# Attention block and mixture of experts on one core: the split of the batches into two expert segments, the spacing of the last stage, the number of padding tiles and the mask of the maxima are changed

## The reference, cut to what matters

```python
# attention: 16 heads of 8 columns, causal
scores = Q @ K.T / sqrt(8);  scores = where(k > q, -1e6, scores)
attn = softmax(scores) @ V
x = layernorm(x + attn @ Wo + bo)
# experts: 8 of them, the best two for each row, hidden width 512
xn = layernorm(x) * gamma + beta
p = softmax(xn @ Wg.T);  top1, top2 with weights p1/(p1+p2), p2/(p1+p2)
y = sum over the two: weight * (gelu(xn @ W1[e] + b1[e]) @ W2[e] + b2[e])
x = layernorm(x + y)
```

## Time and profile before

| what | value |
|---|---|
| median of 3 runs | 992.43 us (990.83 to 999.39) |
| the profiled execution: its time, its span | 994.34 us, 992.5 us |
| PE, DVE, ACT, POOL busy | 88%, 75%, 68%, 66% of the span |
| attention (the scores end) | about 20 to 650 us |
| tiles without the last stage | 658 to 880 us |
| tiles beside the last stage | 880 to 962 us |
| last stage alone | 969 to 992.5 us |

### The profile page before, as it was taken

The page is one execution under the profiler, slowest core; times in us unless marked ns, Lnnn a source line. Parts: engine busy times, 40 slices in busy tenths (PEclk is TensorE's granted clock), DMA queues, the critical chain, the costliest instruction groups (busy, mean ns, idle before and its releaser), DMA issues.

```text
span 992.5 us, 29037 instructions
## 1 busy us (share of the span) xinstructions
PE 873.5 (88%) x9185; PEld 566.2 (57%) x9185; DVE 740.1 (75%) x2029; ACT 677.9 (68%) x1434; POOL 653.6 (66%) x907
## 2 busy tenths in 40 slices
PE   4689899998999989999999999769999999998960
PEld 2334444444444444544444444359999988998860
DVE  1877779888988888888888888855554555458867
ACT  1277687777787777877777877746666555667763
POOL 6243555778678777777787786667767656556652
PEclk9799999999999999999999999989999999999995
DMA  7614635636446355345354342253233323266644
GB/s 198 194 66 158 176 92 165 175 107 203 123 146 203 100 172 167 103 155 171 99 165 147 101 145 61 79 143 87 79 81 89 86 75 89 74 206 193 209 110 146
DMA packets 169379, 132.50 MB, mean 134 GB/s; under 512 B 52938, under 2 KB 155377, under 8 KB 169104
## 3 DMA queue, kind: packets, MB, share of 16 engines
q1 hardware_dynamic: 156880, 112.48, 38.5%
q0 software_dynamic: 8704, 17.06, 5.1%
q10 hardware_dynamic: 3648, 1.12, 0.5%
HBM read 71.55 MB, written 61.15 MB: 134 GB/s over the span
## 4 chain that ended last, share of the span: by engine, by line
PE 37%; POOL 8%; issue 6%; ACT 5%; DVE 5%; DMA 1%; ACTq 1%; SPq 0%; DVEq 0%; POOLq 0%
PE ring L1235 12%; PE ring L1251 11%; PE ps_v L1171 3%; POOL probs L666 2%; PE ring L1108 2%; DVE negmax L1282 2%; ACT probs L798 2%; PE ring L1139 2%; POOL rs L732 1%; POOL rows_d L708 1%; PE ps_v L1225 1%; ACT probs L937 1%; DVE probs L1624 1%; PE ring L1154 1%; ACT vpad L922 1%
## 5 line engine op out<-in xcount | busy, mean ns | idle before, releaser
L1282 DVE TENSOR_REDUCE negmax<-ring 128x2 f32<-128x1024 f32 (+3 forms) x512 | 409.5, 814 | 70.5 <-PE ring L1154 67.5
L798 ACT ACTIVATE probs<-ring 128x768 f32<-128x768 f32 (+1 forms) x384 | 334.7, 878 | 114.0 <-PE ring L1108 107.9
L666 POOL TENSOR_SCALAR_AFFINE_SELECT probs<-probs 128x512 f32<-128x512 f32 x256 | 162.8, 639 | 159.5 <-ACT probs L798 157.7
L922 ACT ACTIVATE vpad<-ring,b_s 128x128 f32<-128x128 f32 x576 | 164.5, 370 | 113.5 <-PE ring L1235 111.1
L716 POOL DMA_INDIRECT y_d<-vpad,xs x144 | 146.3, 1016 | 99.1 <-DVE vpad L1593 54.9
L1171 PE MATMUL ps_v<-probs,vpad 128*32 128x512 f32 (+3 forms) x2048 | 180.2, 441 | 8.3 <-POOL probs L666 8.3
L1235 PE MATMUL ring<-vpad,w_t 128*128 128x128 f32 x1152 | 156.0, 279 | 8.7 <-ACT vpad L945 5.8
L1251 PE MATMUL ring<-qarea,vpad 128*128 x1152 | 155.0, 278 | 3.3 <-issue 3.0
L1235 PEld LDWEIGHTS ring<-vpad,w_t 128*128 128x128 f32 x1152 | 141.7, 194 | 11.1 <-ACT vpad L945 7.2
L708 POOL DMA_INDIRECT rows_d<-xn,slot x128 | 128.6, 1005 | 28.4 <-issue 25.1
L1251 PEld LDWEIGHTS ring<-qarea,vpad 128*128 128x128 f32 x1152 | 140.0, 192 | 7.8 <-issue 6.5
(11 more groups left out here) (190 smaller groups left out, 1170.0 us busy)
## 6 DMA issues: line engine op xcount, KB each, us to landing
kside<-qk_d SPq DMA_DIRECT2D x32, 512.0 KB, 5.5
qk_d<-qarea SPq DMA_DIRECT2D x32, 384.0 KB, 2.7
xs<-rows_d SPq DMA_DIRECT2D x144, 66.0 KB, 1.9
qk_d<-qarea SPq DMA_DIRECT2D x32, 256.0 KB, 2.4
qarea<-qk_d SPq DMA_DIRECT2D x16, 512.0 KB
qodd<-qk_d SPq DMA_DIRECT2D x16, 512.0 KB
probs<-y_d SPq DMA_DIRECT2D x16, 512.0 KB, 4.5
xin<-L_attn_x SPq DMA_DIRECT2D x16, 256.0 KB, 3.8
```

The lines of the kernel that those rows point to most:

```text
L666: pool.affine_select(out=diag, in_=diag, pattern=[[0, 4], [1, P]], compare_op=ALU.is_ge, fill=0.0, base=0, channel_multiplier=-1).then_inc ...
L798: nc.scalar.activation(of_unit(h // 2, part), ring[:, 2 * part % 3, :, (0, P, P)[part]:S], ACT.Exp, scale=SCALE).then_inc(sem("exp_done"), 1)
L922: ins = nc.scalar.activation(ht[:, n % 4, c, :], ps_a[:, n % 4, c * P:(c + 1) * P], ACT.Gelu_apprx_tanh, bias=b1_s[:, bass.ds(e, 1), c:c + ...
L1282: ins = nc.vector.tensor_reduce(negmax[:, n // 6 % 2, qb, s:s + 2], ring[:, (2 * n + 1) % 3, :, c0:c0 + nk], AX.X, ALU.max, negate=True)
```

## The change

It has four parts.

1. `FIRST` is (0, 11, 16) in place of (0, 12, 16): segments of 11 and 5 batches.
2. `TILES` has 7 padding tiles for each segment in place of 8: 88 + 7 = 95 and 40 + 7 = 47, 142 tiles in all, where 104 + 40 = 144 stood.
3. The last stage of batches 0 to 10 starts every 4 steps, from step 95 + 4 = 99; that of batches 11 to 15 every 3 steps, from step 147. The fifth of the late batches uses the buffers of the first of them.
4. Each half of a diagonal block is masked by 64 columns, not 128. The quarter that this leaves out (first 64 queries, second 64 keys) is masked through the spare rows: a row that is 1 for the queries of a first half meets one that is the large negative number for the keys of the same block's second half. `fill` becomes two tiles (in `x2` and `xc`), and their second rows are computed at the start by one iota, three small instructions and two copies. These rows are in both score products.

```diff
-    FIRST = (0, NB - 4, NB)
+    FIRST = (0, NB - 5, NB)
-    TILES = [n * TOPK // P + E for n in SEG]
+    TILES = [n * TOPK // P + E - 1 for n in SEG]
...
-        LAST0, LAST_STEP, LAST_PARTS = TILE0[1] + 4, 3, 12
-        STEPS = range(2 * PAIRS, LAST0 + LAST_STEP * NB + LAST_PARTS)
+        LAST0, LAST_PARTS = TILE0[1] + 4, 12
+        LAST_AT = [LAST0 + 4 * b if b < FIRST[1] else NT + 5 + 3 * (b - FIRST[1]) for b in range(NB)]
+        STEPS = range(2 * PAIRS, LAST_AT[-1] + LAST_PARTS)
...
-            b, rest = divmod(n - LAST0 - part, LAST_STEP)
-            return b if rest == 0 and 0 <= b < NB else None
+            return LAST_AT.index(n - part) if n - part in LAST_AT else None
...
-                             fill[:, :] if what else across(fill[:, 1], 2)).then_inc(sem(f"filled{par}"), 16)
+                             fill[what][:, :]).then_inc(sem(f"filled{par}"), 16)
...
-            sp.wait_ge(sem("fill_set"), 2)
+            sp.wait_ge(sem("fill_set"), 4)
...
-                if b < FIRST[1]:
+                if not FIRST[1] <= b < FIRST[1] + 4:
                     load_x2(b)
...
-                if b is not None and b + 4 < FIRST[1]:
+                if b is not None and (b + 4 < FIRST[1] or FIRST[1] <= b < NB - 4):
                     load_last(b + 4)
                 b = last_stage(n, 3)
-                if b is not None and FIRST[1] <= b + 4 < NB:
+                if b is not None and b < FIRST[1] <= b + 4:
                     load_x2(b + 4)
                 if n == NT + 1:
-                    for b in range(FIRST[1], NB):
+                    for b in range(FIRST[1], FIRST[1] + 4):
                         load_last(b)
...
+            pool.iota(past_i[:, 0], pattern=[[1, 2 * QB]], base=2 * P, channel_multiplier=-2).then_inc(
+                sem("past_rows"), 1)
...
-                        past = pastb[rows, at:at + P]
+                        past = pastb[rows, HALF:P]
                         if n % 3 == 2:
-                            to = to.rearrange("p (a n) -> p a n", n=P)[:, 0:QB:QB - 1, :]
-                            past = past.unsqueeze(1).broadcast_to([HALF, 2, P])
+                            to = to.rearrange("p (a n) -> p a n", n=P)[:, 0:QB:QB - 1, HALF * c:HALF * (c + 1)]
+                            past = past.unsqueeze(1).broadcast_to([HALF, 2, HALF])
                         else:
-                            c1 = (QB - 1 - n % 3) * P
-                            to = to[:, c1:c1 + P]
+                            c1 = (QB - 1 - n % 3) * P + HALF * c
+                            to = to[:, c1:c1 + HALF]
...
-            nc.vector.memset(fill[:, 0], 1.0).then_inc(sem("fill_set"), 1)
-            nc.vector.memset(fill[:, 1], 0.0).then_inc(sem("fill_set"), 1)
+            nc.vector.memset(fill[1][:, 0], 1.0).then_inc(sem("fill_set"), 1)
+            nc.vector.memset(fill[0][:, 0], 0.0).then_inc(sem("fill_set"), 1)
+            dve.wait_ge(sem("past_rows"), 1)
+            nc.vector.tensor_scalar(past_i[:, 1], past_i[:, 0], 2 * HD - 1, None, ALU.bitwise_and).then_inc(
+                sem("past_rows"), 1)
+            dve.wait_ge(sem("past_rows"), 2)
+            for what in range(2):
+                nc.vector.tensor_scalar(past_f[:, what], past_i[:, 1], float(what), NEG if what else 1.0, ALU.is_equal,
+                                        ALU.mult).then_inc(sem("past_rows"), 1)
+            for what in range(2):
+                dve.wait_ge(sem("past_rows"), 3 + what)
+                nc.vector.tensor_copy(fill[what][:, 1].rearrange("p (j n) -> p j n", n=HALF),
+                                      along(past_f[:, what], HALF)).then_inc(sem("fill_set"), 1)
```

More of the change, by code:

```diff
@@ L203, in build_program @@
         flat = probs[:, :, :].rearrange("p r n -> p (r n)")
-        fill = xc[:, :, :].rearrange("p q d -> p (q d)").bitcast(BF16).rearrange("p (r n) -> p r n", r=2)
+        fill = [t[:, :, :].rearrange("p q d -> p (q d)").bitcast(BF16).rearrange("p (r n) -> p r n", r=2)
+                for t in (x2, xc)]
+        past_i = sb("past_i", [P, 2, 2 * QB], I32)
+        past_f = sb("past_f", [P, 2, 2 * QB])
         y_t = flat[:, 0:8 * S].rearrange("p (r n) -> p r n", r=4)
@@ L295, in expert_steps @@
             return (n, n + 1)
-        LAST0, LAST_STEP, LAST_PARTS = TILE0[1] + 4, 3, 12
-        STEPS = range(2 * PAIRS, LAST0 + LAST_STEP * NB + LAST_PARTS)
+        LAST0, LAST_PARTS = TILE0[1] + 4, 12
+        LAST_AT = [LAST0 + 4 * b if b < FIRST[1] else NT + 5 + 3 * (b - FIRST[1]) for b in range(NB)]
+        STEPS = range(2 * PAIRS, LAST_AT[-1] + LAST_PARTS)
+        assert LAST_AT == sorted(set(LAST_AT))
         def copied(n):
```

## The result

| | median | runs | ratio to the kernel before |
|---|---|---|---|
| before | 996.06 us (990.83 to 1001.06) | 20 | |
| changed | 985.1 us (978.84 to 993.68) | 20 | 0.9897, 95% 0.9872 to 0.9922 |

The change brings 10 to 11 us. The forecast was 975, range 966 to 984: too low by 10, and just outside the range. A part of that is the ground it stood on: the three runs that were shown had a median of 992.43, twenty have 996.06. Against these, a forecast of 17.5 us less would have been 978.6; 6.5 us did not come.

The account below looks back on a forecast made before the run. Bounds: a chain of waits through several engines in attention, VectorE's queue beside the last stage. Terms -8.2 - 12.6 + 2.6 + 0.7 = -17.5 took 994.34 us to 976.8; 1.9 lower for the median gave 975, range 966 to 984.

Parts of the forecast that it names:

- What bounds the kernel: Attention: a chain of waits, 38.3 us a batch, 15 of them over GpSimd; beside the last stage: VectorE's queue, W1 copy last.
- Tiles and last stage, -12.6: Tile 99 to the last tile: two tiles fewer and four steps a batch take 82.9 us, not 95.5; 12.6 us less.
- I take 1.95 for all: Tiles beside the last stage: each of 40 steps was priced at 1.95 us, between 1.90 and 1.99.
- the variance's step would be at 1.90: Last stage beside tiles: variance with two factors is shorter than four additions, so its step takes 1.90 us.
- Rival 3: Last stage beside tiles still costs 0.98 us a batch, ScalarE or the wait for factors being late; 983 us, chance 0.10.
- Its mark: Tiles beside the last stage: a step over 2.2 us in each batch would prove the rival of an unchanged last-stage cost.
- The mask, -8.2: Attention: 64-column masks shorten TensorE's pieces on the chain by 0.55 us a batch, over fifteen batches 8.2 us less.
- rival 4: Attention: TensorE's granted clock falls as the mask streams half the columns, making the kernel slower, 1021 us; chance 0.04.
- the clock stayed at 1.00 where TensorE was busy 93%: Attention: reason given against a clock fall, with the change taking only some 5% off TensorE's work.
- Five batches at the end, +2.6: End of the kernel: one more batch at 3.95 us, less 1.3 us now standing in a wait; 2.6 us more.
- Counters, +0.7: Attention: three small VectorE instructions saving counters move from iteration 15 to 14, onto the chain; 0.7 us more.
- The start, 0: Kernel start: five more small VectorE instructions delay the fill transfers by under 1 us, within 12 us of cover; no cost.

Follow-up runs that it names:

- e3: Changed kernel with VectorE copying W1 of tile n+2 directly behind the result of tile n-1, ahead of additions, statistics and factors; ratio 0.9828 to the kernel before.
- e4: Changed kernel without ScalarE's normalising of batches 0 to 10, except four columns, so their output is not computed; ratio 0.9898 to the kernel before.
- e12: Kernel before with W1 of tile n+2 copied directly behind the result of tile n-1; ratio 0.9939 to the kernel before.
- e14: Changed kernel with 128-column masks, each mask product made twice, in units 12 to 14 of a batch's 24; ratio 0.9875 to the kernel before.
- e16: Changed kernel with W1 copied behind the result, normalising moved later, expert loads ahead of the x2 store, doubled 128-column masks in units 12 to 14; ratio 0.9766, 972.83 us.
- e2: Changed kernel with the old 128-column masks and old fill rows; ratio 0.9912 to the kernel before.
- e7: Changed kernel with 128-column masks in all units, the spare rows kept; ratio 0.9957 to the kernel before.
- e1: Kernel before with only the 64-column masks and their spare rows added; ratio 0.9938 to the kernel before.
- e5: Changed kernel with W1 of tile n+2 copied behind the result of tile n-1, and batches 0 to 10 normalised in parts 10 and 11, not 8 and 9; ratio 0.9861.
- e13: Changed kernel run again unaltered, for comparison on the same chip; ratio 0.9907 to the kernel before.
- e10: Kernel before with the expert-weight and padding-tile loads issued earlier, ahead of the store of x2; ratio 0.9935 to the kernel before.
- e15: Changed kernel with expert loads ahead of the x2 store, and 128-column masks with each product made twice in units 12 to 14; ratio 0.9857 to the kernel before.
- e9: Changed kernel with the expert-weight and padding-tile loads issued earlier, ahead of the store of x2; ratio 0.9892 to the kernel before.

## Why the prediction was partly wrong

*What bounds the kernel.* Right for attention: the chain with its GpSimd part, and TensorE's pieces in the rest (undisturbed batches at 37.7 us, as forecast). For the tiles the engine was right (VectorE's queue, the W1 copy last) and e3, e4 and e12 show it.

*Tiles and last stage, -12.6.* This step failed: "I take 1.95 for all". It took the additions, behind which the W1 copy still stood, to be nearly free. The engine was right and the size wrong; the term measured -6.7 in the profile (-6.2 to -8.7 in the eight profiles that have the changed kernel's order of tiles and all of its work).

The 1.95 came from a single step of additions alone, 1.99 us, behind tile 110, which had itself waited 0.92 us. In that wait VectorE had caught up: the copy for the product at 886.64 had ended 0.5 us before it. In the steady state nobody catches up, since TensorE alone needs 1.90. Each step with additions costs what the result, 1.04 us of additions, 0.42 us of copy and the passing on take, and a short step does not give it back. The statement that the variance's step would be at 1.90 failed too: it took 1.94 and 1.90 in the first two batches, then 2.03 to 2.17, though the copy was in time there. Of the 5.9 us, 39 steps of 2.07 are 4.8; the step of 2.88 is 0.9, and the first two are 0.2.

Rival 3 priced this at 0.98 us a batch, and 8.36 - 7.58 = 0.78 us was measured. Its mark, a step over 2.2 us in each batch, held in the first two batches (3.15 and 2.88) and in four others (2.21 to 2.31), and not in the rest. It was nearer than the forecast (90.7 us for T, against 88.8 measured and 82.9 forecast), with the cause on VectorE and not where it was put.

*The mask, -8.2.* Price and mechanism of a piece were right: 0.06 and 0.11 us a piece, 37.7 us a batch. The second pair of products follows the first by 28 ns in the median, where it was 56, and by 56 where it was 109. The Trainium skill, "TensorE: Matmul & The Clock Gate", section "LDWEIGHTS (loading the stationary operand)", with its 107 ns for a load of 128 columns would have kept the pieces as they were, and they halved. A load's own record in these groups is 94 ns long, near that figure, but the product that needs it starts 27 ns behind the load's start: the length of a load is not the distance between products.

What failed is the sum over the batches, and with it the reason against rival 4: "the clock stayed at 1.00 where TensorE was busy 93%". Rival 4 had the right mechanism with the wrong measure on both sides. The share of a 100 us stretch says nothing here. It is the poorest place of a batch that the added work of e14 to e16 mended, where 2.1 to 2.3 of 3.40 us had become 1.84. And the clock does not fall for all batches but in two or three of sixteen, and costs 1.4 to 1.9 us each time.

With the expert loads where they were, A is 463.7 in the mean of four profiles with 128 columns (before, e2, e7, e12) and 461.8 in six with 64 (changed, e1, e3, e4, e5, e13): 1.9 less where 6.6 were forecast for twelve batches. The stretches, two in the mean within A, give back some 3 us of it. The other loss was in no part of the prediction: a batch with late placed maxima takes about 39 to 40 us with either mask, so there the mask's gain turns into a longer wait. These waits between 100 and 600 us are 4.0 us in the mean of the six and 2.4 in that of the four, 1.6 more. That makes 6.6 - 3 - 1.6 = 2.0. The first piece is shown by e14 to e16, the second is read from single profiles that scatter (2.3 to 5.9 us, and 2.0 to 3.0); and since e10 against e15 gives 4.9 in place of the 6.6, the account is good to a microsecond or two and no more.

*Five batches at the end, +2.6*: +2.6. *Counters, +0.7*: the sum left out that they no longer stand in iteration 15. Batch 14 takes 0.4 us more than with the old segments (37.73 against 37.32 in e1; with 128 columns 38.11 in e2 against 37.35), and the maxima of batch 15, from the first to the last, take less (36.74 against 37.02; 36.53 against 37.32). So the term is 0.1 at most. *The start, 0*: the fill transfers leave at 3.50 us and the load behind them is issued at 15.79, against 3.49 and 15.86.

*The ground.* 3.6 of the 10 us lie in the median of the three runs shown, 992.43 where twenty have 996.06: that part of the miss is the luck of three runs and says nothing of the mechanism.

## What to carry to other kernels

When work is spread over more steps of a loop whose bounding engine has no slack, don't take the price of a step from one that follows a wait. Build the loop from one result to the next product, and first put what the next product waits for ahead of what nobody waits for. That one move was worth 7 us here, as much as two tiles and the wider spacing together.

When work is taken off TensorE, look at the place in the period where it already waits most: here the granted clock fell there and gave part of the gain back. Half a microsecond of idle work a batch, laid into a wait, took the falls away and with them 3.5 us of attention; by time the gain is not yet clear of the noise.

Of a kernel that scatters by 10 us, compare stretches of the profiles before the medians, and compare like with like: a profile without late transfers flatters whatever was changed in it.

## What the hardware showed unexpectedly

- TensorE's granted clock fell to half in attention in all seven profiles with 64-column masks everywhere (15 stretches of 3.4 us), and in none of five with 128 columns, although TensorE's work in the poorest place differs by a quarter to half a microsecond (1.84 against 2.1, in one batch shown 2.30, of 3.40 us). The mean clock over all runs, 0.967 to 0.972 against 0.975 to 0.976, points the same way: 0.0045 less of 990 us are 9 us more at half clock. Only a part of this lies in attention, though: of the 23 us that the changed kernel's profile has more at half clock than that of before, 6.8 lie between 60 and 600 us, 3.4 before, 6.9 where attention ends, and 5.8 in the longer end.
- Two pairs of products of 64 columns, each product with a load of 128 columns, take 0.06 us on the chain: the second pair starts 28 ns behind the first (median of 240 groups), though each load's record is 94 ns long and the first loads run beside the products before.
- With 512 KB of weights and two padding tiles (66 KB each) issued 2 to 3 us ahead of 2 MB of others, TensorE waited up to 1.5 us for a 16 KB transfer of another queue; with the loads issued 9 us earlier, and the 2 MB 0.4 to 1.5 us earlier, it hardly did (e9, e10, e15, e16).
